# Query and key stacks with the rows of one dim side by side, no zero rows, in four groups of two batches

## The reference

```python
x = x + tanh(g_xattn) * xattn(layernorm(x), ctx, Wq, Wkv, Wout, bout)
x = x + tanh(g_ffn)   * ffn(layernorm(x), Wg, bg, W1, W2, W3)

# xattn: 8 batches, 256 tokens, 64 context rows ahead of the tokens as keys, 16 heads of 8 dims
q = x @ Wq ; k, v = split(concat(ctx, x) @ Wkv)        # 320 keys
attn = softmax(where(key > token + 64, -inf, q k^T * 8**-0.5))
out = (attn @ v) @ Wout + bout
# ffn: gate, top 2 of 8 experts with a capacity of 320, silu(x W1) * (x W2) @ W3, weighted sum
```

## Time and profile before

| | us |
|---|---|
| median of 3 runs | 278.56 (277.73 to 278.65) |
| the profiled execution: its time | 278.96 |
| the profiled execution: span of its instructions | 277.2 |

### The profile page before, as it was taken

The page is one execution under the profiler, slowest core; times in us unless marked ns, Lnnn a source line. Parts: engine busy times, 40 slices in busy tenths (PEclk is TensorE's granted clock), DMA queues, the critical chain, the costliest instruction groups (busy, mean ns, idle before and its releaser), DMA issues.

```text
span 277.2 us, 6040 instructions
## 1 busy us (share of the span) xinstructions
PE 228.3 (82%) x2233; PEld 145.1 (52%) x2233; DVE 157.7 (57%) x444; ACT 134.1 (48%) x300; POOL 160.7 (58%) x248
## 2 busy tenths in 40 slices
PE   1699968189999999999999999749899999999600
PEld 1587414045666666666666655424466666666400
DVE  6689884236888888888898655530034333433400
ACT  6277205137788786777787774330133333333100
POOL 5665693414756597877868743777004455666552
PEclk9999997858999999999999999997999999999965
DMA  7564388987232234243200020121463556562220
GB/s 197 81 111 114 105 113 97 121 221 169 62 92 73 62 89 121 91 152 121 60 14 22 11 68 12 38 69 41 105 172 79 114 119 140 134 137 26 18 20 5
DMA packets 31157, 24.93 MB, mean 90 GB/s; under 512 B 3859, under 2 KB 28312, under 8 KB 31128
## 3 DMA queue, kind: packets, MB, share of 16 engines
q1 hardware_dynamic: 25536, 19.23, 29.5%
q0 software_dynamic: 4352, 4.71, 9.4%
q10 hardware_dynamic: 1240, 0.61, 0.8%
HBM read 9.27 MB, written 5.82 MB: 54 GB/s over the span
## 4 chain that ended last, share of the span: by engine, by line
PE 57%; DVE 10%; POOL 9%; DMA 9%; issue 7%; ACT 4%; POOLq 1%; SPq 0%; DVEq 0%
PE PS L1209 12%; PE PS L1189 7%; PE PS L1377 7%; PE PS L1379 6%; DMA qst<-mrow 6%; PE PS L1388 6%; POOL places L669 4%; DVE mxb L919 3%; ACT pt L766 3%; PE PS L1148 2%; PE PS L1173 2%; PE PS L1242 2%; PE PS L1165 2%; PE PS L1168 2%; PE PS L1367 1%
## 5 line engine op out<-in xcount | busy, mean ns | idle before, releaser
L766 ACT ACTIVATE pt<-PS 128x512 f32<-128x512 f32 x128 | 71.3, 596 | 40.2 <-PE PS L1189 39.2
L1189 PE MATMUL PS<-qst,kst 64*128 64x192 bf16 (+2 forms) x384 | 48.7, 242 | 14.1 <-DMA qst<-mrow 10.6
L705 POOL DMA_INDIRECT out<-kst x24 | 36.4, 1516 | 41.2 <-DMA out<-kst 18.9
L919 DVE TENSOR_REDUCE mxb<-PS 128x2 bf16<-128x640 f32 x64 | 52.1, 815 | 0.0
L918 DVE TENSOR_REDUCE mxb<-PS 128x2 bf16<-128x384 f32 x64 | 34.8, 543 | 24.9 <-PE PS L1173 24.4
L1189 PEld LDWEIGHTS PS<-qst,kst 64*128 64x128 bf16 x384 | 30.2, 96 | 35.3 <-DMA qst<-mrow 11.6
L1081 DVE TENSOR_TENSOR kst<-PS,kst 128x320 f32<-128x320 f32 x32 | 15.7, 491 | 49.7 <-ACT kst L851 49.7
L669 POOL DMA_INDIRECT places<-rows,dest x32 | 33.1, 1034 | 16.0 <-issue 9.3
L1209 PE MATMUL PS<-pt,vp 128*32 128x256 f32 (+2 forms) x768 | 38.7, 321 | 0.6 <-DVE pt L1040 0.5
L628 POOL TENSOR_SCALAR_AFFINE_SELECT pt<-pt 128x512 f32<-128x512 f32 x28 | 19.0, 677 | 31.2 <-ACT pt L766 31.1
L1148 PE MATMUL PS<-ones 128*128 128x512 bf16 x102 | 28.9, 408 | 0.0
(11 more groups left out here) (141 smaller groups left out, 369.7 us busy)
## 6 DMA issues: line engine op xcount, KB each, us to landing
kp<-in_w SPq DMA_DIRECT2D x24, 256.0 KB, 2.9
kst<-kp SPq DMA_DIRECT2D x18, 160.0 KB, 3.6
qst<-qp SPq DMA_DIRECT2D x18, 128.0 KB, 3.5
places<-blank POOLq DMA_DIRECT2D x8, 162.5 KB, 5.1
kst<-places SPq DMA_DIRECT2D x8, 130.0 KB, 2.4
out<-xs SPq DMA_DIRECT2D x4, 256.0 KB, 2.7
kst<-kp SPq DMA_DIRECT2D x12, 80.0 KB, 2.1
qst<-qp SPq DMA_DIRECT2D x12, 64.0 KB, 2.1
```

The lines of the kernel that those rows point to most:

```text
L705: nc.gpsimd.indirect_dma_start(out=tokens, out_offset=bass.IndirectOffsetOnAxis(ap=ex[0:n, e, s, D:D + 1].bitcast(u32), axis=0), in_=yr[0: ...
L766: nc.scalar.activation(pt[:, U % 2, h, :], PS[:, 4 + h % 2, :], ACT.Exp, scale=SCALE).then_inc(exp_done, 1)
L919: nc.vector.tensor_reduce(mxb[:, U % 2, 1, :, p], PS[:, a:a + 2, 192:512], axis=AX.X, op=ALU.max).then_inc(max_done, 1)
L1189: c = nc.tensor.matmul(PS[:, 4 + par, c0:c1], keys_of(r, gp)[:, g0 + p, i, k0:k0 + 128], queries_of(r, gp)[:, g0 + p, i, q0:N], start=True ...
```

## The change

The stack's partitions are laid out anew. Each parity owns 64 partitions, and in them a row r owns the 8 neighbouring partitions 8r to 8r+7, one for each dim ("64 par + 8 r + d"). The six rows take 48 partitions, the maximum takes one more (`QROW`), and the rest is not used: there are no zero rows. `scores` contracts 48 partitions, `scores_t` 49, in place of 64. One `load_q` or `load_k` is now two transfers, one for each parity, of 8 partitions each. The groups of the stacks (`STACKS`) are four, of two batches each; the groups of the tokens stay. The maxima of a unit are two transfers. The rows of -1 are two transfers of one partition for each group. GpSimd issues the four transfers of q's second part of the first group, and the third parts of batch 1 come ahead of `rstd_of(4)`. The wait for the -1 rows moves from `scores` to `scores_t`. The first four units' maxima are issued by ScalarE, as before.

```diff
+    STACKS = tuple((b, 2) for b in range(0, B, 2))
-    SPAN, MROW, ZROW = 8, 6, 7
+    QROW = 6 * HD
+    KROWS = QROW + 1
-        minus = sb("minus", [2 * HD, 512], bf16)
+        minus = sb("minus", [1, KEYS], bf16)
...
-        def load_q(eng, g, r):
-            b0, n = GROUPS[g]
+        def load_q(eng, g, par, r, landed):
+            row = 64 * par + HD * r
+            b0, n = STACKS[g]
             eng.wait_ge((q1_done, q2_done, q3_done)[QPART[r]], b0 + n)
-            eng.dma_start(queries_of(rows_of(r), g).rearrange("p g b n -> p g (b n)"),
-                          qp[:, QPART[r], b0:b0 + n, :].rearrange("p b n -> p (b n)")).then_inc(stack_in[g], 16)
+            eng.dma_start(queries_of(slice(row, row + HD), g).rearrange("p g b n -> p g (b n)"),
+                          qp[64 * par:64 * par + 64, QPART[r], b0:b0 + n, :].rearrange("p b n -> p (b n)")
+                          ).then_inc(landed, 16)
...
         def load_maxima(eng, U):
             gp, i, g0 = place(U)
             eng.wait_ge(mrow_done, U + 1)
-            eng.dma_start(queries_of(slice(MROW, 128, SPAN * HD), gp)[:, g0:g0 + UP, i, :],
-                          mrow[:, U % 2, :]).then_inc(m_in[U % 2], 16)
+            for par in range(2):
+                row = 64 * par + QROW
+                eng.dma_start(queries_of(slice(row, row + 1), gp)[:, g0:g0 + UP, i, :],
+                              mrow[UP * par:UP * par + UP, U % 2, :]).then_inc(m_in[U % 2], 16)
...
+            def load_minus(g):
+                b0, n = STACKS[g]
+                for par in range(2):
+                    mn = minus[:, :]
+                    sp.dma_start(kst[64 * par + QROW:64 * par + KROWS, b0 * PAIRS * KEYS:(b0 + n) * PAIRS * KEYS]
+                                 .rearrange("p (a k) -> p a k", k=KEYS),
+                                 bass.AP(tensor=mn.tensor, offset=mn.offset,
+                                         ap=[mn.ap[0], [0, n * PAIRS], [1, KEYS]])).then_inc(fixed_in[g], 16)
+
+            sp.wait_ge(consts, 4)
+            load_minus(0)
+            load_part(sp, load_q, QPART, 0, 0, stack_in[0])
+            load_part(sp, load_k, KPART, 0, 0, stack_in[0])
+            load_part(sp, load_k, KPART, 0, 1, stack_in[0])
+            load_part(sp, load_q, QPART, 0, 2, stack_in[0])
+            load_part(sp, load_k, KPART, 0, 2, stack_in[0])
+            load_minus(1)
+            for quarter in (0, 2, 1, 3):
+                load_quarter(sp, 1, quarter)
...
-                if tick == 0:
-                    load_quarter(sp, 2, 3)
-                elif tick < 9:
-                    load_quarter(sp, 3 + (tick - 1) // 4, (tick - 1) % 4)
+                if tick < 8:
+                    load_quarter(sp, 2 + tick // 4, tick % 4)
+                    if tick % 4 == 1:
+                        load_minus(2 + tick // 4)
...
             third_parts(0)
             rstd_of(3)
+            third_parts(1)
             rstd_of(4)
-            third_parts(1)
+            load_part(pool, load_q, QPART, 0, 1, stack_pool)
...
-                if p == 0 and U % 2 == 0 and i == 0:
+                if p == 0 and U % 4 == 0:
                     stacked(pe, gp)
...
-                    pe.wait_ge(m_in[U % 2], 16 * (U // 2 + 1))
+                    pe.wait_ge(m_in[U % 2], 32 * (U // 2 + 1))
+                    pe.wait_ge(fixed_in[gp], 32)
...
-                r = slice(64 * par, 64 * par + 64)
+                r = slice(64 * par, 64 * par + KROWS)
```

More of the change, by code:

```diff
@@ L189, in flamingo_gated_block @@
         vp_set = sem("vp_set")
-        fixed_in = [sem(f"fixed_in{i}") for i in range(2)]
+        fixed_in = [sem(f"fixed_in{g}") for g in range(len(STACKS))]
         consts = sem("consts")
@@ L215, in flamingo_gated_block @@
         v_done = sem("v_done")
-        stack_in = [sem(f"stack_in{g}") for g in range(len(GROUPS))]
+        stack_in = [sem(f"stack_in{g}") for g in range(len(STACKS))]
+        stack_pool = sem("stack_pool")
         s_ready = sem("s_ready")
@@ L374, in place, with load_k, load_part @@
             b = U // 2
[L375 removed]
+            return b // 2, b % 2, UP * (U % 2)
         places = nc.dram_tensor("places", (SLOTS, ROW), fp32, kind="Internal").ap()
         block = es.enter_context(nc.Block())
[L380 to L384 removed]
+        def load_q(eng, g, par, r, landed):
+            row = 64 * par + HD * r
+            b0, n = STACKS[g]
             eng.wait_ge((q1_done, q2_done, q3_done)[QPART[r]], b0 + n)
[L386 to L390 removed]
+            eng.dma_start(queries_of(slice(row, row + HD), g).rearrange("p g b n -> p g (b n)"),
+                          qp[64 * par:64 * par + 64, QPART[r], b0:b0 + n, :].rearrange("p b n -> p (b n)")
+                          ).then_inc(landed, 16)
+        def load_k(eng, g, par, r, landed):
+            row = 64 * par + HD * r
+            b0, n = STACKS[g]
             eng.wait_ge((k1_done, k2_done, k3_done)[KPART[r]], b0 + n)
[L392 to L395 removed]
+            eng.dma_start(keys_of(slice(row, row + HD), g).rearrange("p g b k -> p g (b k)"),
+                          kp[64 * par:64 * par + 64, KPART[r], b0:b0 + n, :].rearrange("p b k -> p (b k)")
+                          ).then_inc(landed, 16)
+        def load_part(eng, load, parts_, g, part, landed):
             for r in range(6):
                 if parts_[r] == part:
[L398 removed]
+                    load(eng, g, 0, r, landed)
+                    load(eng, g, 1, r, landed)
         def load_quarter(eng, g, quarter):
@@ L435, in _ @@
                              wout.rearrange("(v m c) d -> m v c d", v=2, m=UP)[m]).then_inc(small_in, 16)
[L436 to L445, removed]
@@ L475, in store_tokens @@
                 sp.dma_start(x_tiles(out)[:, 4 * g:4 * g + 4, :], xs[:, 4 * g:4 * g + 4, :]).then_inc(stored, 16)
-            for quarter in range(1, 3):
-                load_quarter(sp, 2, quarter)
             for tick in range(UNITS):
@@ L482, in _ @@
                     load_maxima(sp, tick + 1)
-                if tick == 0:
-                    load_quarter(sp, 2, 3)
-                elif tick < 9:
-                    load_quarter(sp, 3 + (tick - 1) // 4, (tick - 1) % 4)
+                if tick < 8:
+                    load_quarter(sp, 2 + tick // 4, tick % 4)
+                    if tick % 4 == 1:
+                        load_minus(2 + tick // 4)
                 if tick == 9:
-                    for g in range(len(GROUPS)):
+                    for g in range(len(STACKS)):
                         stacked(sp, g)
+                        sp.wait_ge(fixed_in[g], 32)
                     load_expert(0)
@@ L519, in _ @@
             nc.gpsimd.memset(half[:, :], -0.5).then_inc(consts, 1)
-            nc.gpsimd.memset(minus[:, :], 0.0).then_inc(consts, 1)
-            for i in range(2):
-                pool.wait_ge(consts, 4 + i)
-                nc.gpsimd.affine_select(out=minus[:, :], in_=minus[:, :], compare_op=ALU.not_equal, fill=-1.0,
-                                        base=-HD * i, pattern=[[0, 512]], channel_multiplier=1).then_inc(consts, 1)
+            nc.gpsimd.memset(minus[:, :], -1.0).then_inc(consts, 1)
             def rstd_of(g):
```

46 lines of the change are left out of this document (16 added, 30 removed).

## The result

The kernel before took 278.61 us (median of 4 runs beside the changed one, 277.73 to 279.78), the changed kernel 286.84 us (4 runs, 285.04 to 290.26). The ratio is 1.027, with a 95% interval of 1.020 to 1.034: it is slower, where I forecast faster. The profiled execution took 285.04 us, its span is 283.3 us against 277.2, so 6.1 us have to be found.

A forecast was written before the change was run, and what follows sets the result against it. Transfers were taken to bound the kernel up to about 57 us, behind that TensorE and VectorE. 5.3 + 0.5 - 2.5 - 7.4 = -4.1 us from 278.96, less 0.4 to the median: 274.5 us; range 266.5 to 288.

The forecast's parts named there:

- The old bound and its cause: Up to about 57 us transfers bound the kernel: the fixed rows delay both units' maxima, 5.97 and 11.15 us to land.
- The issue bound: First group of stack transfers: SP's 20 issues end at 28.0, with 2.1 us to land it is there at 30.1.
- the one by issue: Rival, chance 0.25: eight engines keep up, first scores +0, maxima land in 2.1 us; 267.8 us, range 266.5 to 271.
- The rival of a late first group: Chance 0.20: at 65 GB/s TensorE stands idle from 30.35 to 44.2; +7.0, 285.6 us, range 279.4 to 288.
- I take 95 GB/s, in the middle: Rate of the first group's stack transfers: 18.6 us, ready at 35.6 against 30.35; first scores +5.3 us, bounds 0 and +13.9.
- I take 3.5 us: -2.5 us: Landing of unit 0's maxima with the second group in flight: 3.5 us instead of 5.97, bounds -3.9 and 0.
- 17.1 and 8.2 GB/s: A busy DMA engine's rate before, in 20 to 30 and 44 to 54 us; eight engines give 136 or 65 GB/s.
- Unit 0's maxima: From first scores to unit 0's exponentials: +0.5 us for ScalarE's second issue, -2.5 us for landing; exponentials at 46.2.
- Unit 1's wait: Unit 1 begins about 7.1 us behind unit 0 instead of 14.5, its maxima's landing hidden: -7.4 us.
- I count no difference: TensorE's clock: it now waits at 30 us instead of 50, for less time, so no time is counted.
- its estimated 33: First group's time in us if one transfer runs at the skill page's 54 GB/s; the sum would lose some 18 us.
- the sign of eight engines: In 20 to 45 us a DMA share near 0.5 at most if 8 engines work, near 0.3 if 16.

The follow-up runs named there:

- b1: The kernel before with one line changed: the zero rows are read from partitions 0, 8, 16, ... 120 instead of 0 to 15; ratio 0.975 to the kernel before.
- x4: The changed kernel with a transfer's eight rows 6 partitions apart and one transfer for a unit's maxima instead of two; 267.12 us, ratio 0.960 to the kernel before.
- step 6: The changed kernel with the eight rows of a stack transfer 6 partitions apart instead of adjacent; ratio 0.9741 on one chip, 0.9711 on another, to the kernel before.
- a1: The changed kernel with SP waiting for unit 0's maxima to land before it issues the second group; 3.8% slower than the changed kernel.
- a2: The changed kernel, rows still adjacent, with one transfer for a unit's maxima instead of two; ratio 1.012 to the kernel before.
- x1_again: The second run of step 6, unchanged, on another chip beside the changed kernel; 271.54 us, ratio 0.9711 to the kernel before.
- x5: step 6 with GpSimd's four transfers of the first group issued by SP; median 3.6 us above its base, runs spread too far for a ratio.

## Why the prediction was wrong

**What held.** The old bound and its cause: the second wait for maxima went with the fixed rows, and b1 shows that their slow reading was behind it. The matmuls of 48 and 49 rows cost nothing: from unit 4 on x4 goes from unit to unit in 7.3 to 7.8 us, as the kernel before does. The issue bound (whole at 30.1): step 6, with the same issues, is whole at 30.9. The list of rivals: the one by issue gave 267.8 us, and x4, which is the changed kernel with spread rows and one transfer of maxima, took 267.12. With two transfers, as the rival's sum has them, step 6 took 271.54 and 272.35 us, just above that rival's range of 266.5 to 271. The rival of a late first group gave 285.6 us, and the changed kernel did 286.84, but that is luck in good part: it had the first scores 13.9 us late, not 7.8, and none of the losses behind them.

**The step that failed: how fast the crowded stack transfers are served, in two terms.** Between my -4.1 and the measured +6.2 lie 10.3 us. The first term is "I take 95 GB/s, in the middle": by the same reckoning (1.77 MB from 17 us to 37.9) it was 85 GB/s, and the first scores came +7.8 us late, not +5.3, which is 2.5 of the 10.3. That alone would have left a gain; by my own break-even the first group had to be whole after 39.8 us for a loss, and it was whole at 37.9. The second term is "I take 3.5 us: -2.5 us" for the landing of unit 0's maxima: they took 6.50 us behind the second group's crowded transfers, 3.0 us more. The two together turn the gain into a loss of 1.4. The other 4.8 are 1.3 for the clock, 0.7 for the issue, and 2.5 and 0.3 behind unit 3, all below. Of the two rows for a busy engine, 17.1 and 8.2 GB/s, the slow one was near for 20 to 30 us (9.1) and too slow behind that (12.4 to 15.4). The transfers that gave it read 16 neighbouring partitions; I held that against it as a peculiarity, and it was the property that the new writes share. Why the rate recovers behind 30 us no run shows.

**Unit 0's maxima.** Forecast: +0.5 for the issue and -2.5 for the landing. Measured: +1.2 and +0.5. The landing time of a small transfer depends on what else is under way: 1.64 us in a1, with the second group held back, and 6.50 behind it. I had let the group's slowness into one term and not into the next. The half clock behind the new idle stretch added 1.1 us ahead of the issue and 0.2 behind the landing, neither of which was in the sum (two fillers of 512 columns take 0.97 us, 0.54 in x4).

**Unit 1's wait.** Forecast -7.4, measured -5.5: hidden as foreseen, but unit 0's own work ran at the low clock. "I count no difference" for the clock was wrong by about 1.3 us in this execution: 1.1 + 0.2 + 1.9 lost, and 1.9 given back, since unit 1's work lay in 54 to 64 us at 0.51 before.

**What was not in the sum.** 2.5 us between units 7 and 10. a2 lays them to the second transfer of maxima, by way of TensorE's pause ahead of unit 8's cast and the fall of the clock behind it. In step 6 (x1_again) the step from unit 7 to unit 8 takes 8.3 us and in x4 7.8. Why the second transfer makes the pause, and just there, is open, and so is what brings the clock down.

The sum again: 7.8 + 1.1 + 1.2 + 0.5 + 0.2 - 5.5 - 1.9 + 0.3 + 2.5 = +6.2 us, and the spans differ by 6.1. It is read off one pair of profiles, so that it adds up is no test of it. By experiment the loss has two parts, by ratios to the kernel before: 1.012 - 0.960 = 5.2% is the crowded rows, and 1.024 - 1.012 = 1.2% the second transfer of maxima (this one is small beside the intervals, which touch, 1.016 and 1.015; against the first comparison's 1.027, whose interval begins at 1.020, it is 1.6%, and x4 against its base gives 1.0%). Without both, the change is a gain of 4.0%.

**The pages.** The Trainium skill (SBUF — State Buffer, "Door 1: The DMA port swizzle") was the rule that spoke against this change, and it was right in sign; the first group took 21 us, though, not its estimated 33, and the loss was 6, not 18. By it eight rows 2 apart reach 4 ports, twice as many as adjacent ones; the traces agree (146 GB/s against 89), and show the same for the side that is read (193 against 114). No run separates ports from mere nearness, which rows that share a port without being neighbours would do. Its 54 GB/s for one transfer cannot be read off here, since two halves are always under way together; an estimate of twice that, 108 GB/s, stands among the changed kernel's windows (89, 111, 155, 127), so it is neither borne out nor refuted. The rule of 8 engines (DMA: Bandwidth & Descriptors, "Why a DMA increments its semaphore by 16 and not by 1") fits a share of 0.50 in step 6 from 20 to 30 us, but the changed kernel has 0.61 there, more than the 0.5 that I had named as the sign of eight engines, so the share settles nothing. In step 6 few engines cost nothing that can be seen: 149 GB/s went through.

## What to carry to other kernels

Before rows are packed into adjacent partitions, ask how many transfers will each write (or read) a few neighbours: where transfers followed each other closely, the same bytes spread over partitions moved twice as fast for each busy engine, and the small transfers behind them landed sooner. With half the bytes in each transfer at the same pace, adjacent rows cost nothing (16.8 GB/s for a busy engine). When two rows of a trace bound a rate from both sides, don't take the middle; ask which row has the access pattern and the load to come, and carry the rate through every later term: the landing of unit 0's maxima cost me more than the first group. Cut a transfer in two only with the issue in the sum: 0.52 to 0.65 us on the issuing engine for each.

## What the hardware showed that I had not expected

- Reading from neighbouring partitions is slow as well as writing to them: 114 against 193 GB/s for the same fixed rows.
- Rows 2 partitions apart are already enough at 146 GB/s.
- A transfer of 2 KB issued by another engine's queue still waits for large ones: 1.64 us with no stack transfer under way, 2.28 with spread transfers, 6.50 with crowded ones.
- Keeping TensorE busy with filler through the new idle stretch gave nothing that could be measured (ratio 1.023 against 1.024, each to about 1%).
- TensorE's granted clock can fall to half in a stretch where it is busy almost throughout (0.51 from 116.5 to 120 us, 3.49 of 3.50 us busy), 9 us behind a pause of 1.13 us. Kernels whose longest pause was under 0.5 us did not show it; x5, with a pause of 0.96 us, did not either. The cause is open.
